# A delta-rule block with a quantized feed-forward part: the last inverses applied as three rounded products

## The reference

```
x  = layernorm(x)                                  # plain; the old x is added at the end
d  = layernorm(x, dn_g, dn_b)
q, k, v = split(d @ gates_w + gates_b);  lr = d @ lr_w + lr_b
k  = k / norm(k)
A  = tril(k @ k.T, -1) + I                         # 512 x 512
u  = solve_triangular(A, v, lower=True)
x  = x + ((q @ k.T) @ (lr * u)) @ out_w + out_b
x  = x + relu(layernorm(x, mn_g, mn_b) @ w1 + b1) @ w2 + b2
x  = x_in + x                                      # attention layer with its residual
h  = layernorm(x)
x  = x + (silu(h @ Wg.T) * (h @ Wu.T)) @ Wd.T      # 256 -> 768 -> 256, int weights / 127
```

## Time and profile before

| | us |
|---|---|
| median of 3 runs | 1634.22 |
| lowest and highest run | 1633.17, 1639.21 |
| profiled execution, its own time | 1637.62 |
| span of the profiled execution, first to last instruction | 1635.9 |
| TensorE busy in the span | 1606.2 |
| VectorE, GpSimd, ScalarE busy | 1130.1, 814.5, 776.9 |
| mean granted TensorE clock | 0.994 |
| TensorE busy with the 16 and 8 instructions of L818 and L819 (shift of the weights) | 2.7, 1.9 |

### The profile page before, as it was taken

One profiled execution on the slowest core, in us unless ns is written; L12 is line 12 of the kernel. 1 busy time (PEld: TensorE's weight loads), 2 busy tenths in 40 slices (PEclk: granted clock), 3 DMA queues, 4 the chain that ended last, 5 costly groups with the idle time before them and its releaser, 6 DMA issues.

```text
span 1635.9 us, 30028 instructions
## 1 busy us (share of the span) xinstructions
PE 1606.2 (98%) x10758; PEld 1452.8 (89%) x10758; DVE 1130.1 (69%) x2715; ACT 776.9 (47%) x1501; POOL 814.5 (50%) x1176
## 2 busy tenths in 40 slices
PE   8999999899999999999999999999999999999998
PEld 7899998789999899999898989998989899989987
DVE  5777773477777667777776677777776666666664
ACT  5667664344444444444444444444444444444442
POOL 5556872344444554444445544444444444444441
PEclk9999998899999999999999999999999999999999
DMA  6988998212222222222222222222222222222200
GB/s 214 370 277 284 315 306 269 59 59 72 72 72 72 92 89 71 71 71 72 72 72 87 93 67 71 70 68 70 72 94 73 72 72 71 72 72 72 70 14 27
DMA packets 148588, 178.20 MB, mean 109 GB/s; under 512 B 77781, under 2 KB 130264, under 8 KB 140248
## 3 DMA queue, kind: packets, MB, share of 16 engines
q1 hardware_dynamic: 148440, 176.28, 32.7%
HBM read 98.64 MB, written 77.59 MB: 108 GB/s over the span
## 4 chain that ended last, share of the span: by engine, by line
PE 72%; DVE 7%; POOL 2%; ACT 1%; issue 1%; POOLq 0%; DVEq 0%; ACTq 0%
PE ps L174 27%; PE ps L1060 22%; PE ps L1070 9%; PE ps L980 7%; PE ps L974 4%; PE ps L991 3%; DVE work L1364 2%; DVE bs L1378 2%; POOL sc L1547 1%; DVE wt L1348 1%; DVE work L1371 1%; DVE z_lo L1393 1%; DVE mv L1354 0%; PE ps L246 0%; POOL sc L1550 0%
## 5 line engine op out<-in xcount | busy, mean ns | idle before, releaser
L1596 POOL TENSOR_TENSOR hl<-late,hh 128x512 fp32r<-128x512 f32 x128 | 165.3, 1291 | 206.5 <-ACT hh L1223 206.5
L1070 PE MATMUL ps<-wdT,hh 128*128 128x256 f32 x768 | 203.9, 302 | 0.6 <-ACT late L1218 0.6
L1223 ACT ACTIVATE hh<-late 128x512 fp32r<-128x512 f32 x192 | 120.8, 629 | 163.5 <-DVE late L1388 163.5
L1227 ACT ACTIVATE z_hi<-ps 128x256 fp32r<-128x256 f32 x128 | 48.9, 382 | 296.8 <-PE ps L991 296.8
L1070 PE MATMUL ps<-wdT,hl 128*128 128x256 f32 x768 | 187.1, 281 | 2.0 <-DVE hl L1393 2.0
L1388 DVE TENSOR_TENSOR late<-ps,late 128x512 f32<-128x512 f32 x192 | 132.5, 690 | 74.6 <-PE ps L1060 73.1
L1218 ACT ACTIVATE late<-ps 128x512 f32<-128x512 f32 x192 | 113.6, 592 | 126.1 <-PE ps L1060 126.1
L1578 POOL TENSOR_TENSOR xhm_lo<-xh,xhm_hi 128x1024 fp32r<-128x1024 f32 x32 | 76.4, 2388 | 170.0 <-DVE xhm_hi L1460 170.0
L1060 PE MATMUL ps<-xh3T_hi,wgT 128*128 128x512 f32 x384 | 153.7, 400 | 1.1 <-DVE xh3T_lo L1393 1.1
L1060 PE MATMUL ps<-xh3T_lo,wuT 128*128 128x512 f32 x384 | 152.2, 396 | 0.0
L1060 PE MATMUL ps<-xh3T_lo,wgT 128*128 128x512 f32 x384 | 152.1, 396 | 0.0
(11 more groups left out here) (213 smaller groups left out, 4794.7 us busy)
## 6 DMA issues: line engine op xcount, KB each, us to landing
xhT_scratch<-xhTk SPq DMA_DIRECT2D x32, 1024.0 KB, 7.1
xhT<-xhT_scratch SPq DMA_DIRECT2D x32, 1024.0 KB, 6.2
gg_scratch<-late SPq DMA_DIRECT2D x32, 640.0 KB, 4.2
gg<-gg_scratch SPq DMA_DIRECT2D x32, 640.0 KB, 4.0
xk<-in_L_attn_x_dram SPq DMA_DIRECT2D x32, 512.0 KB, 5.7
xt<-in_L_attn_x_dram SPq DMA_DIRECT2D x32, 512.0 KB, 4.0
out_dram<-late SPq DMA_DIRECT2D x32, 512.0 KB, 2.9
low_scratch<-late SPq DMA_DIRECT2D x128, 16.0 KB, 2.9
```

Of the source, the lines that this page charges most:

```text
L1070: mm = pe.matmul(ps[:, (FG, FU)[j // 2], (j % 2) * C:(j % 2 + 1) * C], part[:, h, blk(j)], wdT[:, h, :], start=(h == 0 and part is hh), st ...
L1223: act.activation(hh[:, h, :], hf[:, h % 2, :], ACT.Copy).then_inc(hh_ev[h], 1)
L1596: pool.tensor_tensor(hl[:, h, :], hf[:, h % 2, :], hh[:, h, :].bitcast(F32), ALU.subtract).then_inc(hl_ev[h], 1)
```

## The change

**z steps.** `pe_zstep` becomes three split products of `xi2` (high part and rest of `x64`, in the memory of the tile m22) and `wt2` (high part and rest of `wt`). ScalarE copies `x64` to `xi2[0]`, VectorE subtracts to get `xi2[1]`. `dve_w` gets two more instructions, a copy and a subtraction, each with a wait for the one before; `wt` shrinks to two alternating buffers. The ready signal of a right hand side (`w_ev`) now comes from the subtraction.

**Order.** TensorE: half of down block 2 ahead of z3 and half behind, the same with down block 3 and z1, z0 behind the transposes t3. VectorE: W 3 and the rest of `xi2` behind h_lo 0; one of the two inversion steps ahead of xh3 is put behind it.

**Norms.** The addition of epsilon goes from GpSimd to VectorE, behind the statistics. The third norm becomes (x - mean) * rstd, so that GpSimd computes only the power. The second has its negated mean from VectorE.

**Last turns.** In turn 33 (`pe_last`) all down products but those of the last hidden block are made first, in four banks; the last output is stored in halves. In turn 32 ScalarE's silu goes ahead of the copy before it, and GpSimd's addition waits for the second norm's transposes to be read.

**Setup.** The biases are added on VectorE to columns in place of products with rows of ones; the key bias comes in another layout; ScalarE issues one activation early; the 128x512 shift of the query and value weights becomes columns that are added as the transposes are evicted.

```diff
+xi2 = [t[:, :, :].rearrange("p k c -> p (k c)").rearrange("p (j c) -> p j c", c=P) for t in m22]
...
-            pe.wait_ge(x128_ev, i + 1)
-            pe.wait_ge(xd_tail, i + 1)
-        pe.matmul(ps[:, A1, 0:C], x64[:, j, :], wt[:, j, :], start=True, stop=True).then_inc(z_ps[j], 1)
+            pe.wait_ge(xi_lo, i + 1)
+        split_matmul(pe, ps[:, A1, 0:C], xi2, [(slice(None), j, slice(None))],
+                     wt2, [(slice(None), j % 2, slice(None))], True, True).then_inc(z_ps[j], 1)
...
+    def pe_last(pe, i):
+        for blocks in (range(HB - 1), (HB - 1,)):
+            for j in range(TB):
+                for h in blocks:
+                    for part, made in ((hh, hh_ev), (hl, hl_ev)):
+                        if j == 0:
+                            pe.wait_ge(made[h], i - 1)
+                        mm = pe.matmul(ps[:, LAST[j], 0:C], part[:, h, blk(j)], wdT[:, h, :],
+                                       start=(h == 0 and part is hh), stop=(h == HB - 1 and part is hl))
+                if j % 2 and h == HB - 1:
+                    mm.then_inc(fo_ps[j // 2], 1)
...
             pe_mlp1(pe, i, 1)
+        if down:
+            after(pe, h1_ev[0], i)
+            pe_down(pe, i, 2, range(HB // 2))
         if att:
             pe_zstep(pe, i, 3)
             pe_weights(pe, i, 4)
             if i == 0:
                 keep_busy(pe, S0, 2)
         if down:
-            after(pe, h1_ev[0], i)
-            pe_down(pe, i, 2)
+            pe_down(pe, i, 2, range(HB // 2, HB))
...
             pe_bt(pe, i, 3)
+        if down:
+            pe_down(pe, i, 3, range(HB // 2))
+        if att:
             pe_zstep(pe, i, 1)
             pe_weights(pe, i, 6)
             if i == 0:
                 keep_busy(pe, S0, 2)
         if down:
-            pe_down(pe, i, 3)
+            pe_down(pe, i, 3, range(HB // 2, HB))
...
-            pe_zstep(pe, i, 0)
...
             pe_transposes(pe, (FO0, FO1), xn, t3_ps)
         if att:
+            pe_zstep(pe, i, 0)
             pe_bt(pe, i, 1)
             pe_bt(pe, i, 0)
...
-                    after(act, z_ps[3], i)
-                    act.activation(wt[:, 3, :], xh[:, 3, :], ACT.Identity, scale=rs[:, i % 2, 2, 3:4],
-                                   bias=zero4[:, 0:1]).then_inc(w_ev[3], 1)
+                    after(act, w_ev[1], i)
+                    act.activation(wt[:, 1, :], xh[:, 3, :], ACT.Identity, scale=rs[:, i % 2, 2, 3:4],
+                                   bias=zero4[:, 0:1]).then_inc(w_f, 1)
         if mlp:
             act_relu(act, i, 0, h12[0], h1_hi)
             act_relu(act, i, 0, h1, h1_ev)
             act_relu(act, i, 1, h12[0], h1_hi)
         act_weights(act, i, range(0, 4))
         if att:
+            act.wait_ge(x128_ev, i + 1)
+            act.wait_ge(xd_tail, i + 1)
+            after(act, y_ps[1], i)
+            act.activation(xi2[0][:, :, :], x64[:, :, :], ACT.Copy).then_inc(xi_hi, 1)
             act_z(act, i, 3)
...
+        if mlp and not att:
+            act_silu(act, i, 0)
+            for h in range(1, HB):
+                act_silu(act, i, h)
+                act_hh(act, i, h - 1)
+            return
...
     def dve_w(dve, i, j):
-        dve.wait_ge(w_ps[j], i + 1)
-        dve.scalar_tensor_tensor(out=wt[:, j, :], in0=xh[:, j, :], scalar=rs[:, i % 2, 2, j:j + 1],
-                                 in1=ps[:, A0, 0:C], op0=ALU.mult, op1=ALU.subtract).then_inc(w_ev[j], 1)
+        if j < TB - 1:
+            dve.wait_ge(w_ps[j], i + 1)
+            dve.scalar_tensor_tensor(out=wt[:, j % 2, :], in0=xh[:, j, :], scalar=rs[:, i % 2, 2, j:j + 1],
+                                     in1=ps[:, A0, 0:C], op0=ALU.mult, op1=ALU.subtract).then_inc(w_f, 1)
+        if j < TB - 2:
+            dve.wait_ge(z_ps[j + 2], i + 1)
+        else:
+            after(dve, z_ps[j - 2], i)
+        dve.wait_ge(w_f, TB * i + TB - j)
+        dve.tensor_copy(wt2[0][:, j % 2, :], wt[:, j % 2, :]).then_inc(w_hi, 1)
+        dve.wait_ge(w_hi, TB * i + TB - j)
+        dve.tensor_tensor(wt2[1][:, j % 2, :], wt[:, j % 2, :], wt2[0][:, j % 2, :].bitcast(F32),
+                          ALU.subtract).then_inc(w_ev[j], 1)
...
+    def dve_eps(dve, n_done, mv_, mvd, ls, done):
+        dve.wait_ge(mvd, n_done)
+        dve.tensor_scalar(ls[:, 0, :], mv_[:, :, 1], EPS, None, ALU.add).then_inc(done, 1)
...
             dve_h1_lo(dve, i, 0)
+        if att:
+            dve_w(dve, i, 3)
+            dve_rest(dve, xi2[1][:, :, :], x64[:, :, :], xi2[0][:, :, :], xi_hi, i + 1, xi_lo)
         dve_invert(dve, m, r, 1, 3)
...
             dve_stats(dve, i, bs3, mv3, bn3, mv3_done)
+            dve_eps(dve, i, mv3, mv3_done, ls3, l3)
         if att:
             dve_z(dve, i, 1)
-        dve_invert(dve, m, r, 3, 5)
+        dve_invert(dve, m, r, 3, 4)
         if mlp:
             dve.wait_ge(ln3_done, i)
+            for k in range(CB):
+                dve.wait_ge(t2_ps[k], i)
             dve_xh3(dve, i, range(2))
         if att:
             dve_w(dve, i, 0)
         if mlp:
             dve_xh3(dve, i, range(2, TB)).then_inc(xh3_done, 1)
+        dve_invert(dve, m, r, 4, 5)
...
+            dve_eps(dve, i + 1, mv2, mv2_done, ls2, l2[0])
+            dve.tensor_scalar(ls2[:, 1, :], mv2[:, :, 0], -1.0, None, ALU.mult).then_inc(l2[1], 1)
...
+    def pool_rstd(pool, n_done, ls, eps_done, sc, done):
+        pool.wait_ge(eps_done, n_done)
+        pool.tensor_tensor(sc[:, 0, :], ls[:, 0, :], mhalf4[:, :], ALU.pow).then_inc(done, 1)
...
+            if not att:
+                for k in range(CB):
+                    pool.wait_ge(t2_ev[k], i)
...
-                pe.matmul(piece(b), diff_bc[:, k, :], wqv[:, k, b * P:(b + 1) * P], start=(k == 0), stop=False)
-            mm = pe.matmul(piece(b), ones[0:1, :], bqv[:, b * P:(b + 1) * P], start=False, stop=True)
+                mm = pe.matmul(ps[:, T0 + 1, b:b + 1], wqv[:, k, b * P:(b + 1) * P], diff[:, k:k + 1],
+                               start=(k == 0), stop=(k == CB - 1))
```

More of the change, by code:

```diff
@@ L349, in setup_act @@
             def setup_act(act):
+                act.wait_ge(ones_set, 1)
+                act.activation(spare[:, :], ones[:, 0:TB], ACT.Identity)
                 act.wait_ge(wkT_ps, 1)
@@ L788, in prep_act @@
                 if q in (2, 3):
+                    act.wait_ge(w_shift_done, 1)
                     act.wait_ge(tq_ps, q - 1)
-                    act.activation(four((wqT, wvT)[q - 2][:, :, :].rearrange("p a b -> p (a b)")), pieces,
-                                   ACT.Copy).then_inc(tq_done, 1)
+                    for o in range(CB):
+                        op = act.activation((wqT, wvT)[q - 2][:, o, :], ps[:, T0 + 1, o * C:(o + 1) * C], ACT.Identity, scale=1.0,
+                                            bias=qcol[:, CB * (q - 2) + o:CB * (q - 2) + o + 1])
+                    op.then_inc(tq_done, 1)
                 if q == 4:
@@ L888, in delta_block_kernel @@
             REST = P - SUB
-            wt = mb("wt", [P, TB, C])
+            wt = mb("wt", [P, 2, C])
+            wt2 = pair("wt", [P, 2, C], c=mc)
             xhm2 = pair("xhm", [P, TB, C], c=mc)
@@ L1413, in dve_out @@
                         after(dve, out_st, i - 2, 16)
+                    if i <= NS:
+                        down = ps[:, (FG, FU)[half], :].rearrange("p (j c) -> p j c", c=C)
+                    else:
+                        down = ps[:, (A0, FO0)[half]:(A0, FO0)[half] + 2, 0:C]
                     dve.scalar_tensor_tensor(
-                        out=ot[:, 2 * half:2 * half + 2, :].rearrange("p j c -> p (j c)"), in0=ps[:, (FG, FU)[half], :],
-                        scalar=QUANT * QUANT, in1=x2s[(i - 1) % 2][:, 2 * half:2 * half + 2, :].rearrange("p j c -> p (j c)"),
+                        out=ot[:, 2 * half:2 * half + 2, :], in0=down, scalar=QUANT * QUANT,
+                        in1=x2s[(i - 1) % 2][:, 2 * half:2 * half + 2, :],
                         op0=ALU.mult, op1=ALU.add).then_inc(ot_ev[half], 1)
@@ L1660, in _ @@
                         sp_body(sp, n)
-                    for n in range(NS - 3, NS):
+                    for n in range(NS - 3, NS - 1):
                         store_out(sp, n)
-                    sp.wait_ge(out_st, 16 * NS)
+                    for half in range(2):
+                        sp.wait_ge(ot_ev[half], NS)
+                        sp.dma_start(out_v[NS - 1][:, 2 * half:2 * half + 2, :], ot[:, 2 * half:2 * half + 2, :]).then_inc(out_st, 16)
+                    sp.wait_ge(out_st, 16 * (NS + 1))
 _INS = ['L0_attn_x', 'L0_attn_dn_g', 'L0_attn_dn_b', 'L0_attn_gates_w', 'L0_attn_gates_b', 'L0_attn_lr_w',
```

84 lines of the change are left out of this document (44 added, 40 removed).

## The result

The changed kernel takes 1885.94 us (median of 4 runs, 1884.79 to 1889.17) beside 1633.70 for the kernel before in the same job: ratio 1.1538, 95% interval 1.1522 to 1.1555. It is slower by 252 us; the forecast was 214 slower. The profiled execution has a span of 1884.1 us against 1635.9.

A forecast was written before the change was run, and what follows sets the result against it. TensorE bound the kernel, with VectorE nearly without slack in the solve. 6.95 us a turn over 31 turns gave 215, +5 and -7 made 213; on 1637.6 that is 1851, 1848 for the median; own range 1815 to 1875, wide 1775 to 1910.

The forecast's parts named there:

- rival 2: Longer TensorE stalls drop the clock: 1952 us if every turn falls, 1900 if half of them; chance 0.12.
- z3: Solve step waiting for xi2's rest, its copy queued behind ScalarE's relu: start at 2.18, stall 1.47 us.
- w2: TensorE's step after z3, waiting for z3's high part and rest out of PSUM: start at 3.73, stall 0.39 us.
- z2: Solve step after the tokens; W 2's copy held by GpSimd's xhm_lo: start at 8.32, stall 2.69 us.
- Rival 1: W 2 before z2 is not held by GpSimd, 1.96 us a turn less: 1787 us; chance 0.17.
- z1 to the transposes: VectorE's stretch from z2 on grows from 7.96 to 9.03 us, so the transposes start at 17.35.
- Gate 0: First gate after the transposes, with z0 and bt0's wait now between: start at 20.65, lag 6.65 us.
- Head of the turn: Second norm's two small VectorE instructions ahead of the last gated product and the mask: 0.3 us more a turn.
- Period: Distance between two casts xhm_hi, one a turn: from 41.15 to about 48.1 us.
- Ends: Outside the 31 periods: turn 0 +5 us; turn 32, turn 33 with the halved store, setup and weights together -7.
- the granted clock stays 1.00: Throughout the turns TensorE keeps its full clock despite the new stalls; nothing added to the sum.
- Rival 3: TensorE stays the bound, new steps fit ScalarE's and VectorE's idle time: 1618 us; chance 0.05.

The follow-up runs named there:

- e3: Changed kernel with ScalarE's copy of x64 to xi2's high part moved ahead of the relu of the second MLP half; 1844.10 us, ratio 1.1289.
- e6: The kernel of e5 with z0 moved behind the transposes t3, down blocks whole; 1665.15 us, ratio 1.0188.
- e5: Kernel before with only the change's norms (inversion step behind xh3 included), last turns and setup; F32 z steps and TensorE's order as before; 1630.71 us, ratio 0.9977.
- e9: The kernel of e5 with the second norm's two small operations back on GpSimd; 1624.54 us, ratio 0.9933.
- e10: Kernel before with only the last turns, the store and the setup new, both norms and the inversion step as before; 1627.71 us, ratio 0.9960.
- e4: Changed kernel with z steps as single F32 products and one-instruction W steps again, no xi2; 1690.00 us, ratio 1.0340.
- e8: The kernel of e4 plus W's copy and subtraction with their waits and two alternating buffers, results used by no product; 1842.44 us, ratio 1.1277.
- e2: Changed kernel with ten unused F32 products on TensorE in front of each z2 of turns 1 to 31; 1868.85 us, ratio 1.1428.
- e7: Changed kernel with the moves of e1 and e3 together; 1768.24 us, ratio 1.0820.
- e1: Changed kernel with W 2 moved ahead of the cast xhm_hi on VectorE; 1803.83 us, ratio 1.1042.

## Why the prediction came out as it did

The sign, the mechanism of the waits and the place of each held; the size was short by 38 us. The time, 1885.94, lies outside the forecast's own range of 1815 to 1875. It fell in the wide range of 1775 to 1910 because that reached over half of rival 2, the falling clock, to which the prediction gave 0.12 and which came about in part; that much is luck. Times count from the same 0 as there, and stalls as there, from where the next product was due.

- **z3.** Forecast at 2.18 with a stall of 1.47: measured at 2.28 and 1.57 (bracket 1.41). The copy behind the relu started at 0.79, as said. e3 removed that order and got 0.96 of the stall back.
- **w2.** Stall 0.39 forecast, 0.39 measured (bracket 0.23).
- **z2.** At 8.32 with the copy held and a stall of 2.69: measured at 8.35 and 2.53 (bracket 2.38). The cast ran 4.51 to 5.20 (forecast 4.43 to 5.12), and the copy took 2.15 against a forecast of over 2. Rival 1 fell.
- **z1 to the transposes.** 17.35 forecast, 17.57 measured; the stall in front of the transposes is 1.52 against 1.5, those of z1 and w0 are 0.24 and 0.37 against 0.2 and 0.4. The norm was shorter by 0.54, forecast 0.49. Here the prediction counted z0's cover as gone, rightly; e6 shows that this and bt0 behind it cost 34 us even when no step is split.
- **Gate 0.** 20.65 forecast, 20.80 measured; the lag is 6.8 against 6.65.
- **Head of the turn.** 0.3 forecast for the second norm; e5 less e9 is 0.28.
- **Period.** 48.1 forecast for a turn at the full clock, 48.35 measured. The 0.25 is 8 us of the miss; 0.15 of it is the lag to gate 0, the rest I have not placed.
- **Idle TensorE.** About 7 us a turn was forecast. The stalls of the turn, bt0's 0.37 with them, add up to 7.0. By busy time the turn from 531.24 has 5.9 us of idle TensorE against 0.05 in the turn from 820.61 before; the difference is the 0.16 of each stall that a record still covers.
- **Ends.** hl in turn 32 is back to 0.69. Outside the 31 periods the change costs 3 us, where +5 and -7 gave -2. e10, with the ends alone, gave 6.5 us, near the 7.

**The step that failed** is "the granted clock stays 1.00", a term that the sum put at nothing. It was argued from one stall of 1.6 us at full clock and from the stalls being split up, and the fall was kept as rival 2 at 0.12. In the changed kernel 18 of the 31 turns were lengthened by it, and five more had a fall of the same length that cost next to nothing. It was also priced too high: 3.35 us per drop from turn 1, where 6.7 us ran at half clock; in these turns 3.4 us did, the products in it lost 1.52, and the period grew by 1.2, since waits behind them took up the rest. This term is 22 us. With the 8 of the period, the 5 of turn 0 and the ends, and the 3.4 that were taken off for the profiled execution of before while that of after lies at its median (1885.95), the 38 are complete.

Rival 3, the bound stays TensorE, asked for xi2's rest 0.71 after the MLP product; it was ready at 2.13. My later theory for e4, that order and norms are a gain by themselves, overlooked the same kind of thing: down blocks and z0 covered waits, and each that was moved left a wait open (0.5 and 0.2 in e6, twice 0.2 more in e4).

## What to carry to other kernels

- When TensorE is busy in over 99% of a stretch and the engine that feeds it at 80%, a step that saves 0.08 us on the first and adds 0.78 on the second is decided on the second: add the new instructions up along the chain to the next start on TensorE, queue places included.
- Put a small SBUF operation of VectorE that is on the critical path ahead of the one that releases a long SBUF instruction of GpSimd: one call moved up gave 82 us here, 64 of them directly.
- An edit bundle that measures as nothing may be a gain and a loss of one size: splitting e5 found the faster kernel.

## What the runs showed of the hardware that was not expected

- The clock falls without TensorE standing still for longer than 2.5 us at a time. In the same program, with the same wait at z2 (2.37 to 2.39 us by the bracket), some turns are lengthened by it and some are not: 18 of 31 in the changed kernel, every second one in e8. With that wait filled (e2) it is 6.
- A fall of 3.4 us costs 1.2 us behind z2 and next to nothing over w2 and the tokens, where the wait for W 2 follows (five turns of the changed kernel).
- Fewer and shorter waits went with fewer falls that cost: 1 us of stall less (e3) halved the slow turns, and with both long ones shortened (e7) there was none behind the second turn. So a stall of this length is worth more than itself: in e1 64 us of waiting removed gave 82. By what rule the clock falls, these runs do not show.
